# A conditioned attention block on one Trainium2 core: the attention output normalised in transposed form, one step later

## What is computed

```python
def _sln(h, w, ln_g, ln_b, Wg, bg, Wb, bb):
    ln = (h - mu) / jnp.sqrt(var + EPS) * ln_g + ln_b
    gamma = (w @ Wg.T + bg)[:, None, :]
    beta = (w @ Wb.T + bb)[:, None, :]
    return gamma * ln + beta
...
h = _sln(hidden, w, ...)                     # hidden 16 x 256 x 256, 16 heads of 16
qkv = (h @ Wqkv.T + bqkv).reshape(B, N, num_heads, hd, 3)
...
energy = jnp.einsum('bhqd,bhkd->bhqk', q, k)
att = jax.nn.softmax(energy, axis=-1) / D ** 0.5
out = jnp.einsum('bhqk,bhkd->bhqd', att, v)
out = jnp.moveaxis(out, 1, 2).reshape(B, N, D)
out = out @ Wp.T + bp
h1 = out + hidden
h2 = _sln(h1, w, ...)
return h2 + h1
```

## Time and profile before

| | us |
|---|---|
| median of 3 runs | 345.21 |
| lowest, highest | 345.2, 345.9 |
| the profiled execution, whole | 345.56 |
| its span, first to last instruction | 343.8 |
| TensorE busy | 332.5 |
| VectorE busy | 298.3 |
| ScalarE busy | 242.8 |
| GpSimd busy | 159.1 |

### The profile page before, as it was taken

The page is one execution under the profiler, slowest core; times in us unless marked ns, Lnnn a source line. Parts: engine busy times, 40 slices in busy tenths (PEclk is TensorE's granted clock), DMA queues, the critical chain, the costliest instruction groups (busy, mean ns, idle before and its releaser), DMA issues.

```text
span 343.8 us, 8981 instructions
## 1 busy us (share of the span) xinstructions
PE 332.5 (97%) x3173; PEld 286.8 (83%) x3173; DVE 298.3 (87%) x728; ACT 242.8 (71%) x476; POOL 159.1 (46%) x187
## 2 busy tenths in 40 slices
PE   8888999999999999999999999999999999999993
PEld 4677879888888988888888988888898988888773
DVE  4888978799898989899898989989898988999684
ACT  7664876868676786868686876868687786766740
POOL 5765544437164545527264644617254643224330
PEclk9999999999999999999999999999999999999999
DMA  7396445456555454555545454655556354652021
GB/s 242 126 218 186 124 115 140 129 155 157 170 141 156 134 152 135 173 156 170 142 125 169 134 155 134 184 142 160 161 135 157 98 157 123 182 146 67 16 61 61
DMA packets 47705, 48.87 MB, mean 142 GB/s; under 512 B 6287, under 2 KB 41374, under 8 KB 47662
## 3 DMA queue, kind: packets, MB, share of 16 engines
q1 hardware_dynamic: 44494, 46.74, 49.2%
q10 hardware_dynamic: 1184, 1.07, 1.2%
q0 software_dynamic: 1984, 0.51, 0.8%
HBM read 9.99 MB, written 4.23 MB: 41 GB/s over the span
## 4 chain that ended last, share of the span: by engine, by line
PE 87%; DVE 5%; DMA 3%; ACT 1%; issue 1%; ACTq 1%; SPq 0%; DVEq 0%
PE m L976 24%; PE st L976 19%; PE sa L976 18%; PE pv L976 17%; PE pv L1065 4%; DVE mx L692 3%; PE pv L1146 2%; PE m L1105 2%; DMA wqkv<-WqkvT_dram 2%; DMA kst<-qk_l 1%; PE pv L1079 1%; PE m L1079 1%; ACT p L602 0%; DVE qk_l L727 0%; ACTq L625 0%
## 5 line engine op out<-in xcount | busy, mean ns | idle before, releaser
L692 DVE TENSOR_REDUCE mx<-sa 128x2 f32<-128x512 f32 x256 | 171.5, 684 | 28.4 <-PE sa L976 27.3
L602 ACT ACTIVATE p<-st 128x512 f32<-128x512 f32 x240 | 140.9, 598 | 37.5 <-PE st L976 33.2
L976 PE MATMUL sa<-kst,qst 126*128 126x256 f32 x512 | 105.6, 288 | 2.0 <-DMA kst<-qk_l 1.0
L976 PE MATMUL st<-qst,kst 128*128 128x256 f32 x496 | 104.1, 292 | 0.2
L976 PEld LDWEIGHTS st<-qst,kst 128*128 128x128 f32 x496 | 75.1, 188 | 13.8 <-issue 12.8
L976 PEld LDWEIGHTS sa<-kst,qst 126*128 126x128 f32 x512 | 78.6, 189 | 4.6 <-DVE mx L692 1.7
L368 POOL DMA_DIRECT2D qst<-m_h x31 | 17.6, 567 | 112.4 <-DVE m_l L701 112.4
L976 PE MATMUL pv<-p,v_st 128*32 128x256 f32 x1008 | 61.0, 382 | 0.0
L976 PEld LDWEIGHTS pv<-p,v_st 128*32 128x32 f32 x1008 | 29.5, 109 | 21.0 <-ACT p L602 1.5
L976 PE MATMUL m<-hT_h,wqkv_h 128*128 128x256 f32 x128 | 36.8, 300 | 1.3 <-ACT hT_h L616 0.7
L377 POOL TENSOR_SCALAR xn<-xa,mv,rstd 128x256 f32<-128x256 f32 x28 | 34.2, 1227 | 1.5
(11 more groups left out here) (149 smaller groups left out, 566.2 us busy)
## 6 DMA issues: line engine op xcount, KB each, us to landing
qst<-qk_h SPq DMA_DIRECT2D x64, 128.0 KB, 2.4
qst<-qk_l SPq DMA_DIRECT2D x64, 128.0 KB, 2.5
kst<-qk_h SPq DMA_DIRECT2D x62, 128.0 KB, 2.5
kst<-qk_l SPq DMA_DIRECT2D x62, 128.0 KB, 2.8
xa<-x_dram SPq DMA_DIRECT2D x16, 256.0 KB, 3.0
gb<-gb_rows SPq DMA_DIRECT2D x16, 256.0 KB, 3.9
out_dram<-y SPq DMA_DIRECT2D x15, 256.0 KB, 3.4
wqkv<-WqkvT_dram SPq DMA_DIRECT2D x1, 512.0 KB, 5.6
```

Source lines behind the costliest of these rows:

```text
L602: nc.scalar.activation(p32[:, h, :], st_ps[h % 2][:], ACT.Exp).then_inc(exp_done, 1)
L692: dve.tensor_reduce(mx[:, par(a), h // HH, (h % HH) * TT:(h % HH + 1) * TT], sa_ps[h % 2][:].rearrange("p (t n) -> p t n", t=TT), AX.X, AL ...
L976: return nc.tensor.matmul(o, l, r, start=start, stop=stop)
```

## The change

For batches 0 to 13 (`by_transfer`) the output stays transposed. SP's `send_out(a, g)` copies from `oT` the rows of sums (one of each head, 8 KB, spread over 64 partitions of the tile `sums`) and the rows of output (128 KB, into `o_rows`, which reuses the weight tile `wqkv`). VectorE takes one `reciprocal` of `sums` in slot 6. SP's `gather_rec` (two transfers of 16 KB) puts the reciprocals into 16 rows of `recs` (in tile `wb`) and `spread_rec` (256 KB) spreads them to the partitions of `o_rec` (tile `wg`). VectorE's `normalise(a)` multiplies rows and reciprocals in slot 3 of step a+2, ScalarE casts `aT_h` in slot 4 (`high_att`), GpSimd subtracts `aT_l` (`low_att`), and the projection is that of batch b-2. So 12 transposes for each of the 14 batches are gone, and the residual of a batch comes one step later (b-3). Batches 14 and 15 still go by tokens (`normalise_tokens`), and the projection of batch 13 stands in the last step. V's columns alternate with ones, and the rows of Wp and the V bias are permuted to fit. The twelve products of a projection are ordered so that the low parts come last. On GpSimd `xn` comes early in the step and the two powers are instructions of their own (slots 15 and 5); x's statistics move on VectorE from slots 4 and 5 to 11 to 13, for batch b+4, with a seventh buffer for x. `evict_out` of group 0 moves from slot 12 to 14.

```diff
-S_MT1, S_AT, S_MT0, S_XT = 1, 10, 9, 10
+S_MT1, S_AH, S_MT0, S_XT = 1, 4, 9, 10
...
-NX = 6
-S_O1, S_O0 = 3, 12
-S_OT1, S_OT0 = 6, 14
+NX = 7
+S_O1, S_O0 = 3, 14
+OUT_PRODUCTS = [(l, r, k, t) for l, r in ((0, 0), (0, 1), (1, 0)) for k in range(2) for t in range(2)]
...
-        att = sb("att", [P, TT, D])
+        sums = sb("sums", [P, H * N // P])
+        recs = wb[0:2 * HH].rearrange("p k n -> p (k n)")
+        o_rows = [wqkv[:, :, D:2 * D], wqkv[:, :, 2 * D:3 * D]]
+        o_rec, att = wg, wqkv[:, :, 0:D]
...
+        def by_transfer(a):
+            return 0 <= a < B - 2
...
+            def send_out(a, g):
+                if not by_transfer(a):
+                    return
+                half_rows = slice(g * P // 2, (g + 1) * P // 2)
+                sp.wait_ge(oT_ready, 2 * a + g + 1)
+                wait(sp, recs_in, 32 * a)
+                sp.dma_start(sums[half_rows, :], oT[1:P:32, g, :]).then_inc(sums_in[g], 16)
+                wait(sp, aTh_ready, a - 1)
+                wait(sp, aTl_ready, a - 1)
+                sp.dma_start(o_rows[par(a)][half_rows], oT[0:P:2, g, :].rearrange("p (c n) -> p c n", c=2)).then_inc(o_in[g], 16)
+            def gather_rec(a):
+                if not by_transfer(a):
+                    return
+                sp.wait_ge(rec_ready, a + 1)
+                for n in range(2):
+                    sp.dma_start(recs[n:2 * HH:2, :], sums[:]).then_inc(recs_in, 16)
+            def spread_rec(a):
+                if not by_transfer(a):
+                    return
+                sp.wait_ge(recs_in, 32 * (a + 1))
+                wait(sp, rows_ready, a)
+                sp.dma_start(o_rec[:], recs.rearrange("r (d n) -> r d n", d=1)
+                             .broadcast_to([2 * HH, HD // 2, 2 * N])).then_inc(rec_in, 16)
...
             def step(b):
                 if has(b - 1) or has(b) and not first(b):
                     stack(b + 1, 1)
+                send_out(b - 1, 1)
                 if has(b + 4) and has(b):
                     wait(sp, xn_ready, 1 * (b + 2) + 1)
-                    wait(sp, h1_ready, 1 * (b - 2) + 1)
+                    wait(sp, h1_ready, 1 * (b - 3) + 1)
                     sp.dma_start(xbuf(b + 4), x_t[b + 4]).then_inc(x_in[(b + 4) % 4], 16)
+                gather_rec(b - 1)
                 if has(b):
                     stack(b + 2, 0)
+                spread_rec(b - 1)
...
-                if has(b - 1):
-                    wait(sp, y_ready, 1 * (b - 3) + 1)
-                    if first(b - 1):
+                if has(b - 2):
+                    wait(sp, y_ready, 1 * (b - 4) + 1)
+                    if first(b - 2):
                         sp.wait_ge(gb_out, 16)
-                    sp.dma_start(gb[:, par(b - 1)], gb_dram[b - 1].rearrange("(a n) -> a n", a=1)
-                                 .broadcast_to([P, 2 * D])).then_inc(gb_in[par(b - 1)], 16)
-                if has(b - 2):
-                    wait(sp, y_ready, 1 * (b - 2) + 1)
-                    sp.dma_start(out_t[b - 2], y[:, par(b - 2)]).then_inc(y_out[par(b - 2)], 16)
+                    send_gb(b - 2)
+                if has(b - 3):
+                    send_y(b - 3)
+                send_out(b, 0)
...
+            def low_att(a):
+                wait(pool, aTh_ready, a + 1)
+                pool.tensor_tensor(aT_l[:], o_rows[par(a)], aT_h[:], ALU.subtract).then_inc(aTl_ready, 1)
...
                 for h in range(H):
-                    if h == 5 and has(b):
-                        one, two = has(b + 3), has(b - 2)
-                        if one:
-                            wait(pool, v_step, 3 * (b + 3) + 3)
-                            wait(pool, xn_ready, 1 * (b + 3))
-                        if two:
-                            wait(pool, ln2_step, 4 * (b - 2) + 3)
-                            wait(pool, y_ready, 1 * (b - 2))
-                        which = slice(0 if one else 1, 2 if two else 1)
-                        pool.tensor_tensor(rstd[:, which], vare[:, which], minus_half[:, which],
-                                           ALU.pow).then_inc(rstd_ready, 1)
+                    if h == 0 and has(b - 1):
+                        add_bias(b - 1)
+                    if h == 1 and has(b) and has(b + 3):
+                        norm_x(b + 3)
+                    if h == 4 and by_transfer(b - 2):
+                        low_att(b - 2)
+                    if h == 5 and has(b - 3):
+                        rstd_out(b - 3)
...
-                    if h == 5 and has(b + 3) and has(b):
-                        norm_x(b + 3)
-                    if h == 0 and has(b - 1):
-                        add_bias(b - 1)
+                    if h == 6 and has(b - 3):
+                        add_beta(b - 3)
+                    if h == 15 and has(b + 4):
+                        rstd_x(b + 4)
...
                 wait(act, pv_done, 2 * a + g + 1)
-                wait(act, o_done, 2 * (a - 1) + g + 1)
+                wait(act, sums_in[g], 16 * a)
+                wait(act, o_in[g], 16 * a)
                 nc.scalar.activation(oT[:, g, :], pv_ps[g][:], ACT.Copy).then_inc(oT_ready, 1)
+            def high_att(a):
+                wait(act, rows_ready, 1 * a + 1)
+                wait(act, proj_done, 1 * (a - 1) + 1)
+                nc.scalar.activation(aT_h[:], o_rows[par(a)], ACT.Copy).then_inc(aTh_ready, 1)
...
+            def reciprocal(a):
+                if not by_transfer(a):
+                    return
+                for g in range(2):
+                    wait(dve, sums_in[g], 16 * (a + 1))
+                dve.reciprocal(sums[:], sums[:]).then_inc(rec_ready, 1)
+            def normalise(a):
+                if not by_transfer(a):
+                    return
+                for g in range(2):
+                    wait(dve, o_in[g], 16 * (a + 1))
+                wait(dve, rec_in, 16 * (a + 1))
+                dve.tensor_tensor(o_rows[par(a)], o_rows[par(a)], o_rec[:], ALU.mult).then_inc(rows_ready, 1)
...
                 between = {
                     (2, 1): [lambda: low_max(b, 1)],
-                    (3, 0): [lambda: residual(b - 2, 0), lambda: residual(b - 2, 1)],
-                    (4, 0): [lambda: residual(b - 2, 2), lambda: norm1(b + 3, 0)],
-                    (4, 1): [lambda: residual(b - 2, 3), lambda: norm1(b + 3, 1)],
-                    (5, 0): [lambda: norm1(b + 3, 2)],
+                    (3, 0): [lambda: residual(b - 3, 0), lambda: residual(b - 3, 1), lambda: normalise(b - 2)],
+                    (4, 0): [lambda: residual(b - 3, 2)],
+                    (4, 1): [lambda: residual(b - 3, 3)],
                     (5, 1): [lambda: low_qk(b + 2, 0, m0, qh_ready, ql_ready)],
-                    (7, 0): [lambda: normalise(b - 1, 1, 0)],
+                    (6, 0): [lambda: reciprocal(b - 1)],
                     (7, 1): [lambda: low_qk(b + 2, 1, m1, kh_ready, kl_ready)],
-                    (8, 0): [lambda: normalise(b - 1, 1, 1)],
-                    (9, 1): [lambda: residual(b - 2, 4)],
-                    (11, 0): [lambda: low_max(b + 1, 0), lambda: low_att(b - 1), lambda: residual(b - 2, 5)],
-                    (15, 0): [lambda: normalise(b, 0, 0)],
-                    (15, 1): [lambda: normalise(b, 0, 1)],
+                    (9, 1): [lambda: residual(b - 3, 4)],
+                    (12, 1): [lambda: norm1(b + 4, 1)],
+                    (13, 1): [lambda: norm1(b + 4, 2)],
+                    (10, 1): [lambda: low_max(b + 1, 0), lambda: residual(b - 3, 5)],
+                    (11, 0): [lambda: norm1(b + 4, 0)],
                 }
+                if b == B - 2:
...
             steps(step)
+            residual(B - 4, 0)
+            low_max(B - 1, 1)
+            normalise(B - 3)
+            for stage in (1, 2, 3):
+                residual(B - 4, stage)
+            residual(B - 4, 4)
+            last_out(B - 2, 1)
+            normalise_tokens(B - 2, 1)
+            residual(B - 4, 5)
             residual(B - 3, 0)
-            low_max(B - 1, 1)
-            for stage in (1, 2, 3):
-                residual(B - 3, stage)
-            last_out(B - 2, 1)
-            normalise(B - 2, 1, 0)
-            normalise(B - 2, 1, 1)
             last_high_att(B - 2)
             low_att(B - 2)
...
-            def project_out(quarter):
-                t, k = quarter // KT, quarter % KT
-                o = parts(m1[:, t * D:(t + 1) * D], aT_h[:, k, t * P:(t + 1) * P],
-                          aT_l[:, k, t * P:(t + 1) * P], wp_h[:, k, :], wp_l[:, k, :], k)
+            def project_out(a, quarter):
+                for n in range(3 * quarter, 3 * quarter + 3):
+                    l, r, k, t = OUT_PRODUCTS[n]
+                    if n == 0:
+                        wait(pe, aTh_ready, a + 1)
+                    if n == 8:
+                        wait(pe, aTl_ready, a + 1)
+                    o = mm(m1[:, t * D:(t + 1) * D], (aT_h, aT_l)[l][:, k, t * P:(t + 1) * P], (wp_h, wp_l)[r][:, k, :],
```

(14 more changed lines are left out.)

151 lines of the change are left out of this document (87 added, 64 removed).

## The result

The change makes the kernel **slower: 364.48 us** (median of 4 runs, 362.74 to 367.54) against 345.55 us before (4 runs, 345.2 to 347.52), a ratio of 1.0545, 95% interval 1.046 to 1.063. Forecast were 330.7 us and a range of 327.0 to 337.5. The profiled execution took 367.54 us, the slowest of the four, with a span of 365.7, 21.9 more than the 343.8 before. Executions of one kernel differ by up to some 2%: medians are of all of them, ratios leave out those over 1.5% above the fastest.

What follows compares the result with a forecast made beforehand. The prediction took TensorE as the bound, VectorE 1.65 us behind. Its terms, 16.4 + 0.2 + 2.0 + 0 - 2.1 - 2.0 = 14.5 us, off 345.56 and 0.35 lower for the median, gave 330.7 us, range 327.0 to 337.5.

Steps and rivals of the forecast that it cites:

- TensorE's terms: Twelve transposes fewer per step save 1.37 us in each of steps 2 to 13, 16.4 us; step 1 gives 2.0 more.
- VectorE's sum: VectorE's work per step falls by a net 1.06 us, to 16.8 of 18.13 us, at no cost.
- rival (d): Slot 3's product meets a GpSimd operation and runs late, 0.2 to 0.6 us a step: 335.5 us, chance 0.04.
- (c): VectorE becomes the bound, with waits for maxima in slots 11 to 13 paying back half the saving: 339.1 us, chance 0.07.
- SP and the transfers: Seven more issues per step at 0.59 us, 4.1 us, bring SP to 16.4 of 18.1 us at most.
- the margin of 0.9 us for the sums: Group 1's sums land 8.4 us after slot 15 starts, 0.9 us before VectorE asks for them.
- The landing: Group 1's sums were to land 2.0 us later, by the nearest small transfer.
- rival (e): Sums of group 1 stand behind a whole stack on SP, stopping VectorE at the reciprocal: 352 us, chance 0.03.
- Stalls: -2.0: Late landings of the second stack, 0.5 us in one step of three, cost 2.0 us; possible range 0 to 6.
- The spread "is hidden": The spread of reciprocals lands some 3.8 us before the product in slot 3 needs it.
- Tail: -2.1: Last step: batch 13's projection costs 1.41 us, VectorE's later work some 0.4, waiting for both products 0.3.
- the signs: What would show the forecast right or wrong; wrong if SP's second stack ends over 16.5 us after slot 15 starts (T15).

Runs made afterwards that it cites:

- w2: The changed kernel with SP's list reordered, reciprocal in slot 8, and gathers (slot 9), spread, y and rows of group 1 issued by GpSimd: 336.05 us, ratio 0.9735.
- z4: The changed kernel with gathers and spread issued by GpSimd and the spread alone carrying one eighth of its bytes: 340.27 us, ratio 0.985.
- y4: The changed kernel with gathers, spread, y, and sums and rows of group 1 issued by GpSimd, order kept: 347.76 us, ratio 1.0075.
- z1: y4 with rows and spread carrying one eighth of their bytes: 340.84 us, ratio 0.9867.
- x3: The kernel before with seven more transfers per step on SP, in the change's shapes and places, into tiles nobody reads: 349.6 us, ratio 1.0106.
- x2: The changed kernel with VectorE's reciprocal two slots later, in slot 8: 362.76 us, ratio 1.0487.
- y1: The changed kernel with gathers (slot 7) and spread (slot 12) issued by GpSimd in place of SP: 348.56 us, ratio 1.0065.
- y2: The changed kernel with gathers, spread and y issued by GpSimd in place of SP, order kept: 349.48 us, ratio 1.0099.
- u2: The changed kernel with all issues still on SP, but in a new order and with the reciprocal in slot 8: 354.43 us, ratio 1.0257.
- w1: u2's order and reciprocal, with gathers (slot 9), spread and y issued by GpSimd: 340.41 us in four runs, ratio 0.9846.
- x4: The changed kernel with as many transfers and pieces, but rows and spread carrying one eighth of their bytes: 342.58 us, ratio 0.9891.
- x5: The kernel before with only the four small transfers per step (twice 8 KB, twice 16 KB) added on SP: 346.49 us, ratio 1.0024.
- z3: y4 with the reciprocal in slot 8 and the gathers in slot 9: 346.86 us, ratio 1.0047.

## Why the prediction was wrong

**TensorE's terms: right, a little high.** 1.37 us a step were forecast. An undisturbed step of w2 takes 18.24 where before it took 19.50: 1.26. Over the twelve steps the forecast without stalls was 17.0, w2 shows 14.6. The smaller saving is 1.3 of the difference, and steps of 18.6 and 18.9 us, with a wait in them, most of the rest. Ahead of step 1 the forecast was 1.1 and w2 gained 0.9.

**VectorE and GpSimd: no bound, as forecast, but VectorE's sum was off.** The product takes 0.68 us (forecast 0.70) and the reciprocal 0.35 (0.25); GpSimd has 11.11 us a step (11.1). VectorE has 17.59 where 17.85 - 1.06 = 16.8 were forecast. Of the missing 0.8 us, 0.65 is one instruction that got longer, by what looks like the mechanism of rival (d) at a place that the prediction didn't look at. VectorE's row in the changed kernel, and GpSimd's:

```profile
156.43 0.82 DVE L885 TENSOR_SCALAR vare<-mv 128x2 f32<-128x2 f32 x1
```

```profile
155.92 1.30 POOL L468 TENSOR_TENSOR aT_l<-wqkv,aT_h 128x512 fp32r<-128x512 f32 x1 [1.34 <-ACT aT_h L614]
```

`vare` took 0.16 us in every step before, takes 0.81 in each step now that has an `aT_l` beside it, and ends at 157.25, when GpSimd's `aT_l` ends (157.22); in w2 again at 164.65 and 164.62. The product itself in slot 3 is not lengthened. The Trainium skill has this (SBUF — State Buffer, section Who interferes with whom): a VectorE `tensor_scalar` can be in a mode that takes the port pair shared with GpSimd, and whichever starts second is blocked for the whole instruction; both rows agree. The prediction used the half of that rule on two SBUF inputs and left out this one. It costs 0.65 us of VectorE and, in z4 and w2, nothing of the step, but in y4 and z1, where it took 1.35, TensorE waited (above). So (c) and (d) as priced didn't happen. (d)'s own case, two operations with both inputs in SBUF beside a GpSimd addition, came in the tail: the pair `y<-h,mv,gb` took 1.95 us in the changed kernel and 1.47 in w2, against 1.11 before.

**SP and the transfers: the step that failed.** "SP is at 16.4 of 18.1 us at most": it is 18.5 us of issuing, 1.4 of gaps and 0.6 of waits. Three parts. First, seven issues at 0.59 us were 4.1, and the list grew by 6.6 (by 6.3 in x3). The seven take 4.4 of that; 1.5 is y's issue behind the spread and gb, which the sum had at no more than before, and 0.8 the stacks'. The earlier trace rows had the warning, a single issue of 1.55 us, and it was used as an accident of one step instead of a price that grows with the bytes under way. Second, the gap behind every issue, 0.05 to 0.1 us, was left out: 1.4 us. Third, the 16.4 was called a maximum and the list was not replayed over a whole step. The text begins both loops at T15 with the two issues of group 0 (0.9 us, less than twice its own 0.59) and names nothing in front of them. By its own times the spread, gb and y behind the second stack would just have been out by then. Measured, the second stack of the step before ended at 167.88, 0.7 us ahead of T15 in place of 2.3, and y's issue took 2.06 us in place of 0.34. These two are 3.3 us, the difference between the 4.2 at which the stack started and the forecast 0.9. With it the margin of 0.9 us for the sums turned into a wait of 1.9 us on average, 2.8 in the step shown. The second stack was late too (below), but TensorE, itself held up by the maxima, hardly waited for it; in x2, without the wait for sums, it did.

**The landing: right, and beside the point.** The text let rival (e) begin "once the landing takes over 3.2 us"; it took 1.95, as the 2.0 of the earlier trace rows. What was late is the issue. The mechanism of (e) was named with its place and its sign and was given 0.03, for a cause that didn't happen, and was not tied to the length of the list, which did.

**Stalls: -2.0.** Waits of TensorE, nearly all on maxima, cost about 2 us a step on average, 20.23 against w2's 18.25, so 24 us in twelve. The 0 to 6 us took landings as the only unknown.

**The spread "is hidden":** its landing is (4.6 us). Its bytes aren't: between y1 and z4 they are worth 8 us (z4's interval is wide, 0.973 to 0.997).

**Tail: -2.1.** After the weighing of step 14 w2 loses 3.9 us and the changed kernel 5.7. In w2 its silent end (below) is 1.6 us shorter than before, so the work takes 5.6 longer. VectorE in the same stretch of the kernel before:

```profile
312.46:343.80 31.34, 25.85 (x262) 20.14 (x261) 21.93 (x61) 13.81 (x29) 10.54 (x12) 1.00 0.18 52
```

21.93 us there, 26.13 in the last window of w2 above. The second residual is 4 us of VectorE's work, for which the prediction counted 0.4; that it lies on the path unhidden fits the sums, but no run takes it out. In the changed kernel the lower clock adds to it: 1.1 us in the weighing of step 14 and, between 358.40 and the last matmul, 1.4 us against the same matmuls of w2.

**What was right of the signs:** the statement that the forecast fails if the second stack ends more than 16.5 us after T15. It ended at 188.14, 19.5 us after.

Ahead of step 1 the changed kernel lost 2.4 us where 1.1 were to be gained. Most of it belongs to this execution: x2, whose program is the same up to there, has the weighing of step 0 at 43.42 in place of 45.43, and of these 2.0 us the lower clock from 34.0 to 37.4 is 1.2. Still open: why the clock fell there, where TensorE's waits were short (0.5 us, and 0.3 in x2), and w2's 1.8 us between steps 13 and 14, in which TensorE waits once for `kst`, 2.0 us. The 0.2 us a step of x3 and the price of a large issue are measured, what holds the issue isn't: it could be room in the queue or the DMA engines' own backlog.

## What to carry to other kernels

A queue that only issues transfers is an engine with a busy share of its own. Sum its list as (issues x measured time + gap + waits), take large transfers at the price they have when others are under way, and when the sum comes within 10% of the step, replay it from where it really stands, not from idle. Moving four issues to a second engine was worth 14 to 15 us here (changed kernel to y2, u2 to w1), putting those that somebody waits for ahead of the others 9 to 10 (changed kernel to u2, y2 to w1), and only together did they turn a change that costs 19 us into one that saves 5 (w1). The 9 us of w2 are the same steps with a shorter end, of which more below.

## What was not expected of the hardware

**An issue can wait for bytes of another engine's transfer.** y's issue takes 0.34 us at the median before and 2.02 in the changed kernel, where it stands behind spread and gb (2.06 at 169.25). In u2, where y stands ahead of the spread, it takes 0.45, and in x4, with one eighth of the bytes, 0.43. With the spread on GpSimd's queue SP's issues still took 2.3 us a step too much, with one eighth of its bytes 0.7.

The Trainium skill (DMA: Bandwidth & Descriptors, section Issuing engines are not separate DMA queues) says that starting transfers from several engines only saves the sequencer's time, "which is usually small relative to the DMA itself". The first half agrees: the share of the DMA engines is 0.72 to 0.73 in y1 against 0.66 to 0.70. The second doesn't settle it here: 0.6 us of 2.6 is small for one transfer, and 26 of them are nearly the whole step.

**The end of the program has a silent piece that differs from kernel to kernel.** From VectorE's last instruction to the end of the span it takes 3.9 us before, 2.3 in the changed kernel and in w2, 7.1 and 8.4 in the two profiles of w1, 7.8 in y1 and z4. It repeats to 0.1 us among before, x3 and x5, among y4, z1 and z3, and between y1 and z4, but not between the two of w1. Some 2 us of it are the landing of the last transfer of y; in w1 no engine and no DMA engine works from 333 us to the end at 338.6. VectorE's last rows in w2 (span 334.0) and in the second profile of w1 (span 338.6):

```profile
330.83 0.87 DVE L1090 SCALAR_TENSOR_TENSOR y<-y,rstd,m 128x256 f32<-128x256 f32 x2 [0.63 <-PE m L1096]
```

```profile
330.59 0.87 DVE L1081 SCALAR_TENSOR_TENSOR y<-y,rstd,m 128x256 f32<-128x256 f32 x2 [1.99 <-PE m L1087]
```

They end within 0.3 us of one another, and the spans differ by 4.6. So w2's lead over w1, 4.4 us, is this end, in these two executions, and can't be put down to the rows moved. No run here shows what it is; a difference of this size between two versions should be looked for there first.
